# Eight batches of a transformer kernel: hardware loop on each engine, or the same body written out eight times

## The chip, the cores and the metric

The kernel runs on one core of a Trainium2 chip. The metric is device microseconds (us) of one execution, lower is better. Runs shown are several executions of the same program; one more execution was profiled and gives the trace.

## The reference, cut to what matters

Eight independent batches of 256 queries (128 features) pass through two layers. The first layer is a cross-attention over a context of 1601 rows and a mixture of nine experts, of which two are taken per query; the second is a cross-attention over 64 gathered context rows per query and a mixture of eight experts, of which two are taken, plus a shared one.

```
x = x + xattn0(layernorm(x), ctx)             # softmax over 1601 keys, 16 heads of 8
x = x + ffn0(layernorm(x))                    # 9 experts, hidden 352, top 2 by sigmoid
x = x + xattn1(layernorm(x), ctx, indices)    # softmax over 64 gathered keys
x = x + ffn1(layernorm(x))                    # 8 experts, hidden 176, top 2, and a shared one
```

The two attentions and the two mixtures are the same for every batch, with the same weights. Nothing flows from one batch to the next.

## The kernel before, in words

The program is written by hand for five instruction streams: `@block.sync` (SP, it only issues DMAs and keeps the books), `@block.tensor` (PE), `@block.scalar` (ACT), `@block.vector` (DVE) and `@block.gpsimd` (POOL). Each stream has a preamble that loads and transposes the weights and prepares batch 0, and then a loop of eight passes (`Fori(0, NB)`, L334, L767, L944, L1208, L1343), one batch a pass. Every pass has the same instructions at the same tiles; only SP's body uses the loop's index, for addresses in HBM (the inputs of the batches after this one, L338 and L342, and the output of this one, L353).

Within a pass PE does, in order: the row maxima of the first attention against all 1601 keys (`max_part`, L455, two matmuls a part, each part read by a DVE reduction, L1054), transposes of the next batch's context among them (`context_T`, L541), scores and weighting (L477, L493), counts of the gathered indices (`count`, L550, many tiny matmuls), the first mixture (`experts`, L673), the second attention, the second mixture. The inputs of the next batch are prepared within the pass, so the next pass can begin at once with `max_part`. `keep_clock` (L397) issues matmuls whose result nobody reads, where PE would otherwise be idle; the last four of a pass stand at L803.

The passes are tied together by a meeting. The semaphores only count upward within a pass and are compared with constants, so they are cleared once a pass. PE, ACT, DVE and POOL each call `meet` at the end of a pass (L804, L953, L1225, L1356): drain the engine, add one to `met`, wait for the own `go` semaphore. SP waits in `close` (L318) for the last loads and for `met` to reach four, clears the semaphores and raises the four `go`. Before `close`, SP issues the store of the batch (L353), which it may do once DVE has added the last residual (L1171). After `go`, each engine clears its own `go` and then meets the loop's closing instructions: add one to a register, compare, branch back to the head of the body. The same `meet` and `close` stand once ahead of the loop (L332, L766, L943, L1207, L1342), and there the engines run on into the body without a backward branch.

```
def meet(eng, k):
    eng.drain().then_inc(met, 1)
    eng.wait_ge(go[k], 1)
    eng.sem_clear(go[k])
```

Of the kernel before, what the change touches and what calls it, by code (L numbers as in the profile page):

```python
# [28 lines left out]
NB, NQ, D = 8, 256, 128  # L29
# [39 lines left out]
def build(nc, x, ctx_in, itok, Wq, bq, Wkv, bkv, Wo, bo, w1, w2, w3, nw1, nw2, nw3, gw, ngw, gb,  # L69
# [6 lines left out]
    with ExitStack() as es:  # L76
# [135 lines left out]
# [5 lines that stand above are left out]
# [39 lines left out]
        def _(sp):  # L256
            def load_x(b):
                sp.dma_start(xs[0][:, :, :], x[b].rearrange("a (s p) d -> p (a s) d", p=P)).then_inc(x_in, 16)
                sp.dma_start(idx_i[:, :, :], itok[b].rearrange("a (s p) k -> p (a s) k", p=P)).then_inc(idx_in, 16)

            def load_ctx(b):
                sp.dma_start(ctx_sb[:, 0:KC - 1, :],
                             ctx_in[b, 0:(KC - 1) * P, :].rearrange("a (c p) d -> p (a c) d", p=P)).then_inc(ctx_in_s, 16)
                sp.dma_start(ctx_sb[0:KLAST, KC - 1, :],
                             ctx_in[b, (KC - 1) * P:NK, :].rearrange("a k d -> (a k) d")).then_inc(ctx_in_s, 16)

            def spread(parts, scratch, dst, done, filled, ready):

                for t in range(3):
                    sp.wait_ge(ready, t + 1)  # L270
                    sp.dma_start(scratch[t], parts[t]).then_inc(done, 16)

                    sp.wait_ge(done, 16 * (t + 1))
                    src = scratch[t].rearrange("(a h d) k -> h d a k", h=2, d=HD)
                    for hh in range(2):
                        for term in range(NT):
                            if KPART[term] == t:
                                r = SLOT * hh + HD * term
                                sp.dma_start(dst[r:r + HD, :, 0:src.shape[3]], src[hh]).then_inc(filled, 16)
# [38 lines left out]
            def close():  # L318

                sp.wait_ge(kst_in, 16 * 2 * NT)  # L320
                sp.wait_ge(k1st_in, 16 * 2 * NT)
                sp.wait_ge(x_in, 16)
                sp.wait_ge(idx_in, 16)
                sp.wait_ge(ctx_in_s, 32)
                sp.wait_ge(met, 4)
                sp.sem_clear(round_sems)  # L326
                for g in go:
                    sp.sem_inc(g, 1)
# [2 lines left out]
            sp.wait_ge(ctx_in_s, 64)  # L331
            close()  # L332
            sp.sem_inc(out_stored, 16)
            with sp.Fori(0, NB) as i:  # L334
                nxt = bass.ds((i + 1) % NB, 1)

                sp.wait_ge(ctxT_ready, 4)
                load_ctx(bass.ds((i + 2) % NB, 1))  # L338

                sp.wait_ge(x_ready, 1)  # L340
                sp.wait_ge(cnt_psum, 1)
                load_x(nxt)  # L342

                sp.wait_ge(out_stored, 16)
                sp.sem_clear(out_stored)
                sp.sem_inc(xo_free, 1)

                sp.wait_ge(att_done, 1)
                spread(kpart, k_parts, kst, kw_done, kst_in, kp_ready)
                sp.wait_ge(att_done, 2)  # L350
                spread(kpart1, k1_parts, k1st, kw1_done, k1st_in, kp1_ready)
                sp.wait_ge(x_ready, 4)
                sp.dma_start(out[bass.ds(i, 1)].rearrange("a (s p) d -> p (a s) d", p=P), xs[4][:, :, :]).then_inc(out_stored, 16)  # L353
                close()
# [41 lines left out]
        def _(pe):  # L396
# [111 lines left out]
            def attention0():  # L508
                done = [0]

                def parts(upto):
                    while done[0] < min(upto, NH0):
                        max_part(done[0])
                        if 1 <= done[0] < START:
                            keep_clock(2, ob[:, :])
                        done[0] += 1
                for g in range(4):
                    parts(START + 2 * (g - CTX))
                    context_T(g)
                parts(START)  # L520
                pe.wait_ge(ctxT_ready, 4)
                for kind, n in fills0:
                    if kind == "q":
                        pair_queries(n, fill0[kind, n], m_ready, b_ready, b_read)
                    elif kind == "c":
                        if n == NP - 1:
                            for g in range(NP * NG - LAG, NP * NG):
                                weigh(g)
                            pe.wait_ge(part_read, NH0)
                            keep_clock(2)  # L530
                        combine(n, fill0[kind, n], oT_ready, b_ready, b_read)
                    elif n % 2 == 0:
                        g = n // 2
                        scores(g)
                        x = KC * (g // NG) + chunks(g % NG)[-1] + 1
                        parts(min(START + x * (PARTS + LEAD - START) // KC, LEAD + x * PARTS // KC))
                        if g >= LAG:
                            weigh(g - LAG)
                pe.drain().then_inc(att_done, 1)
# [224 lines left out]
            project(1, attT, wq_sb[:, :], True)  # L764
            all_queries(1, 0)
            meet(pe, 0)  # L766
            with pe.Fori(0, NB):  # L767
                attention0()
                keep_clock(2)
                count(0, COUNT[0])  # L770
                attend_T(0)
                keep_clock(2)
                count(COUNT[0], COUNT[1])
                attend_out(0, wo_sb[:, :])
                keep_clock(4)
                count(COUNT[1], COUNT[2])
                keep_clock(4)
                norm_T(1, False)
                keep_clock(2)
                count(COUNT[2], COUNT[3])  # L780
                experts(0)
                next_values(0, 2)
                mask_T()
                next_values(2, 4)
                norm_T(2, False)
                keep_clock(2)
                project(2, xnT, wq1T[:, :], False)
                keep_clock(8)
                all_queries(1, 1)
                keep_clock(3)  # L790
                attention1()
                keep_clock(3)
                attend_T(1)
                keep_clock(2)
                attend_out(1, wo1T[:, :])
                next_latent1()
                next_keys1()
                keep_clock(10)
                norm_T(3, False)
                keep_clock(2)  # L800
                experts(1)
                pe.wait_ge(hu_done[1], NC1)
                keep_clock(4)  # L803
                meet(pe, 0)  # L804
# [3 lines left out]
        def _(act):  # L808
# [132 lines left out]
            next_keys1()  # L941
            all_queries(0, 0)
            meet(act, 1)  # L943
            with act.Fori(0, NB):  # L944
                next_context()
                attention0()
                experts(0)
                next_values()
                attention1()
                next_keys1()  # L950
                experts(1)
                all_queries(2, 0)
                meet(act, 1)  # L953
# [3 lines left out]
        def _(dve):  # L957
# [247 lines left out]
            scale_queries(1, 0, st)  # L1205
            high_parts(st).then_inc(qres_ready, 1)
            meet(dve, 2)  # L1207
            with dve.Fori(0, NB):  # L1208
                st = Steps(dve, dve_step)
                attention0()  # L1210
                st.do(normalise(0, 0, H - 2, st))
                attend_out(0, x0b, xs[1], st)
                norm(1, xs[1], st)
                experts(0, xs[1], xs[2], st)
                norm(2, xs[2], st)
                scale_queries(1, 1, st)
                st.link(high_parts(st))
                low_parts(st)
                attention1(st)
                st.do(normalise(1, 0, H - 4, st))  # L1220
                st.do(normalise(1, H - 4, H - 2, st))
                attend_out(1, xs[2], xs[3], st)
                norm(3, xs[3], st)
                experts(1, xs[3], xs[4], st)
                meet(dve, 2)  # L1225
# [3 lines left out]
        def _(pool):  # L1229
# [110 lines left out]
            next_indices()  # L1340
            low_parts()
            meet(pool, 3)  # L1342
            with pool.Fori(0, NB):  # L1343
                st = Steps(pool, pool_step)
                attention0(st)
                rstd_of(1)
                next_keys()
                rstd_of(2)
                attention1(st)
                rstd_of(3)  # L1350
                next_keys1()
                next_x()
                rstd_of(4)
                next_indices()
                low_parts()
                meet(pool, 3)  # L1356
# [25 lines left out]
```

## Time and profile before

| | us |
|---|---|
| median of 3 runs | 1911.24 |
| lowest and highest run | 1907.75, 1912.42 |
| the profiled execution, its own time | 1908.32 |
| span of its trace, first to last instruction | 1906.5 |
| mean granted TensorE clock | 0.96 of full |
| body entered | 109.88 |

The profiled execution is 1.8 us longer than its span: that is what lies around the traced instructions. The trace has 36401 instructions. PE is the matmul part of TensorE and PEld its weight loads; SPq is the sequencer of SP. In the chain that ended last, "issue" is time for which the trace shows nothing that the engine waited for. The queues named "instruction" carry the code of the engines from HBM. The eight batches fill the span from 109.88 us to its end.

### The profile page before, as it was taken

The numbers are of one execution on the slowest core, as the hardware profiler recorded it, in microseconds if no ns is written. First come the engines' busy times: TensorE is split into PE (matmuls) and PEld (weight loads), VectorE is DVE, ScalarE is ACT, GpSimd is POOL, SyncE is SP. The second block draws the span as 40 slices with busy tenths as digits, with TensorE's granted clock in tenths as the row PEclk, the third lists the DMA queues.
The fourth block names the chain that finished last, engine by engine and source line by source line (L and its number), as shares of the span: only waits on it lengthen the run. The fifth ranks groups of instructions, "written<-read, shape, count | busy, mean of one in ns | idle before, by whom it ended". The sixth has DMA issues, their size and how long they took to land.

```text
span 1906.5 us, 36401 instructions
## 1 busy us (share of the span) xinstructions
PE 1667.5 (87%) x13858; PEld 905.6 (48%) x13858; DVE 1210.9 (64%) x2626; ACT 899.7 (47%) x2024; POOL 629.7 (33%) x1059
## 2 busy tenths in 40 slices
PE   4159998889988999899997899889998899989999
PEld 3113655237452474435652274534744346533655
DVE  4058555867468664795667764685747856578555
ACT  4138433572427534384335834276342753448433
POOL 3325223441324314352233513243142522335223
PEclk8679999899999999899999999999998999989999
DMA  7410130002200041000400022000311004000130
GB/s 207 76 32 2 30 53 17 19 2 49 35 17 19 6 65 26 24 2 18 66 13 22 2 41 44 17 19 6 59 22 33 2 6 75 17 23 2 30 54 16
DMA packets 56192, 60.30 MB, mean 32 GB/s; under 512 B 6437, under 2 KB 44209, under 8 KB 55985
## 3 DMA queue, kind: packets, MB, share of 16 engines
q1 hardware_dynamic: 55984, 57.57, 15.4%
q8 instruction: 127, 2.08, 0.4%
q14 instruction: 81, 0.66, 0.1%
HBM read 43.67 MB, written 13.88 MB: 30 GB/s over the span
## 4 chain that ended last, share of the span: by engine, by line
PE 69%; DVE 10%; issue 7%; ACT 6%; POOL 4%; DMA 3%; SPq 1%; another core or an unknown queue 0%; POOLq 0%
PE ob L700 7%; PE ob L503 7%; PE b L488 6%; PE a L687 6%; PE a L688 6%; PE a L464 4%; PE a L401 4%; PE b L473 4%; DVE mx L1054 3%; PE ob L401 3%; PE a L583 3%; PE a L582 3%; ACT probs L848 2%; PE b L694 2%; DMA k_parts<-big 2%
## 5 line engine op out<-in xcount | busy, mean ns | idle before, releaser
L1054 DVE TENSOR_REDUCE mx<-a 128x2 f32<-128x802 f32 (+1 forms) x512 | 497.8, 991 | 164.6 <-PE a L464 153.4
L848 ACT ACTIVATE probs<-b 128x512 f32<-128x512 f32 (+1 forms) x896 | 452.9, 567 | 50.1 <-PE b L488 43.3
L503 PE MATMUL ob<-probs,vaug 128*9 128x256 f32 (+1 forms) x3328 | 279.6, 389 | 17.7 <-ACT oT L810 17.7
L917 ACT ACTIVATE big<-a 128x256 f32<-128x256 f32 (+2 forms) x304 | 116.7, 384 | 304.7 <-PE a L688 304.0
L1276 POOL TENSOR_TENSOR big<-iotab,idx_lo 128x512 bf16<-128x512 bf16 x256 | 258.0, 1039 | 5.0
L464 PE MATMUL a<-kst,qa 64*128 64x401 bf16 (+1 forms) x1024 | 180.4, 359 | 74.6 <-SPq L326 42.4
L488 PE MATMUL b<-sq_nat,kst 64*128 64x256 bf16 (+1 forms) x1664 | 174.3, 282 | 20.0 <-ACT probs L848 9.6
L1146 DVE SCALAR_TENSOR_TENSOR big<-big,a 128x256 f32<-128x256 f32 (+2 forms) x304 | 127.1, 418 | 85.2 <-ACT big L917 84.0
L1265 POOL CAST qst<-nm 128x4 bf16<-128x4 f32 x64 | 12.8, 200 | 434.5 <-DVE nm L1038 434.5
L1232 POOL TENSOR_TENSOR rstd<-veps,neg_half 128x2 f32<-128x2 f32 x33 | 23.2, 704 | 361.1 <-DVE veps L965 361.1
L488 PEld LDWEIGHTS b<-sq_nat,kst 64*128 64x128 bf16 (+1 forms) x1664 | 51.4, 96 | 184.8 <-ACT probs L848 171.7
L401 PE MATMUL a<-identb 128*128 128x512 bf16 x496 | 133.5, 380 | 1.7
L1140 DVE TENSOR_TENSOR probs<-big,b 128x256 f32<-128x256 f32 (+2 forms) x304 | 125.8, 414 | 0.6
L1154 DVE TENSOR_TENSOR big<-big,a 128x256 f32<-128x256 f32 (+2 forms) x304 | 125.7, 413 | 0.0
L1066 DVE TENSOR_REDUCE mx<-a 128x4 f32<-128x1024 f32 x64 | 78.4, 1225 | 72.9 <-PE a L583 72.9
L700 PE MATMUL ob<-w2T,probs 128*128 128x128 f32 (+1 forms) x800 | 122.8, 276 | 1.6
L687 PE MATMUL a<-xnT,w1T 128*128 128x256 f32 (+1 forms) x400 | 121.2, 385 | 0.0
L503 PEld LDWEIGHTS ob<-probs,vaug 128*9 128x9 f32 (+1 forms) x3328 | 55.4, 88 | 137.8 <-ACT probs L848 55.8
L688 PE MATMUL a<-xnT,w3T 128*128 128x256 f32 (+1 forms) x400 | 119.0, 379 | 0.0
L700 PEld LDWEIGHTS ob<-w2T,probs 128*128 128x128 f32 (+1 forms) x800 | 105.3, 191 | 25.4 <-DVE probs L1140 4.7
L464 PEld LDWEIGHTS a<-kst,qa 64*128 64x128 bf16 x1024 | 52.2, 100 | 134.0 <-issue 97.0
L1288 POOL TENSOR_TENSOR probs<-probs,cntT 128x512 f32<-128x512 f32 x64 | 81.1, 1267 | 103.6 <-ACT probs L866 102.8
(220 smaller groups left out, 2655.7 us busy)
## 6 DMA issues: line engine op xcount, KB each, us to landing
kst<-k_parts SPq DMA_DIRECT2D x108, 200.1 KB
k_parts<-big SPq DMA_DIRECT2D x27, 400.2 KB, 14.2
ctx_sb<-in_ctx SPq DMA_DIRECT2D x10, 768.0 KB
k1st<-k_parts SPq DMA_DIRECT2D x108, 32.0 KB
k_parts<-kpart SPq DMA_DIRECT2D x27, 64.0 KB, 1.8
kst<-in_L_ffn_w SPq DMA_DIRECT2D x1, 1408.0 KB
x<-in_x SPq DMA_DIRECT2D x9, 128.0 KB, 2.1
out<-x SPq DMA_DIRECT2D x8, 128.0 KB, 1.8
```

Source lines behind the costliest of these rows:

```text
L401: pe.matmul(bank, identb[:, :], identb[:, :].unsqueeze(1).to_broadcast([P, 4, P]), start=True, stop=True)
L464: m = pe.matmul((a0, a1)[k % 2][:, hh * MMAX:hh * MMAX + n], qa[o:o + SLOT, p, s, :], kst[o:o + SLOT, p, j * KM:j * KM + n], start=True, s ...
L488: m = pe.matmul(bs[e[hh] % 3][0:kn, (c % 2) * NQ:(c % 2 + 1) * NQ], kst[o:o + SLOT, p, c * P:c * P + kn], qp[o:o + SLOT, p % 2, :], start= ...
L503: m = pe.matmul(ob[q:q + V1, 0:NQ], vaug[0:kn, c, 2 * p + hh, :], probs[0:kn, (2 * g + hh) % NPS, (c % 2) * NQ:(c % 2 + 1) * NQ], start=(j ...
L687: pe.matmul(gu_bank[c % 3][0:n, 0:NQ], wga[:, c * P:c * P + n], xnT[:, :], start=True, stop=True)
L688: pe.matmul(gu_bank[c % 3][0:n, NQ:2 * NQ], wua[:, c * P:c * P + n], xnT[:, :], start=True, stop=True).then_inc(gu_ready[l], 1)
L700: m = pe.matmul(ob[:, s * P:(s + 1) * P], hid[0:n, c % 4, s * P:(s + 1) * P], wda[0:n, c, :], start=(c == 0 and s == 0), stop=(c == nch - ...
L848: act.activation(probs[0:kn, n % NPS, 0:w], bs[e % 3][0:kn, 0:w], ACT.Exp).then_inc(b_read, 1)
L1054: dve.tensor_reduce(mx[:, p % 2, s, :, j], (a0, a1)[k % 2][:, :].rearrange("p (h k) -> p h k", h=2)[:, :, 0:n], AX, ALU.max, negate=True). ...
L1140: dve.tensor_tensor(hid[0:n, c % 4, :], hu[0:n, c % 3, :], cb_bank[c % 2][0:n, 0:NQ], ALU.mult).then_inc(hid_ready[l], 1)
L1146: dve.scalar_tensor_tensor(out=gt[0:n, c % 3, :], in0=th[0:n, c % 3, :], scalar=1.0, in1=g[0:n, 0:NQ], op0=ALU.add, op1=ALU.mult).then_inc ...
L1276: m = pool.tensor_tensor(onehot[:, q:q + QG, :], iotab[:, :].unsqueeze(1).to_broadcast([P, QG, P]), idx_lo[:, q:q + QG].unsqueeze(2).to_br ...
```

## The change

The five hardware loops become Python loops at build time. The body of each engine's loop stands eight times in a row in its instruction stream. The order of instructions, the tiles, the semaphores, the meeting and its clearing stay. On SP the index is now a number known at build time, so the addresses of the input and output DMAs are constants.

```diff
@@ sync
-            with sp.Fori(0, NB) as i:
+            for i in range(NB):
                 nxt = bass.ds((i + 1) % NB, 1)
@@ tensor
-            with pe.Fori(0, NB):
+            for _ in range(NB):
                 attention0()
@@ scalar
-            with act.Fori(0, NB):
+            for _ in range(NB):
                 next_context()
@@ vector
-            with dve.Fori(0, NB):
+            for _ in range(NB):
                 st = Steps(dve, dve_step)
@@ gpsimd
-            with pool.Fori(0, NB):
+            for _ in range(NB):
                 st = Steps(pool, pool_step)
```

## Rows read from the trace of the kernel before

**Rows 1.** The page, part 1: busy time of each engine over the span.

```profile
PE 1667.5 (87%) x13858; PEld 905.6 (48%) x13858; DVE 1210.9 (64%) x2626; ACT 899.7 (47%) x2024; POOL 629.7 (33%) x1059
```

**Rows 2.** Windows, one per batch (2, 5, 8) and all eight: length, busy times, clock.

```profile
335.41:561.09 225.68, 205.30 (x1713) 110.42 (x1714) 148.62 (x323) 109.11 (x248) 74.61 (x127) 0.97 0.13 26
...
1009.34:1233.12 223.78, 203.70 (x1712) 110.11 (x1713) 148.43 (x323) 109.02 (x248) 74.61 (x127) 0.98 0.14 26
...
1683.76:1906.50 222.74, 205.23 (x1712) 110.44 (x1712) 148.63 (x323) 109.10 (x248) 74.61 (x127) 0.98 0.13 26
sum 1796.62, PE 1638.74 PEld 882.80 DVE 1188.17 ACT 872.62 POOL 596.86; mean PE 204.84 PEld 110.35 DVE 148.52 ACT 109.08 POOL 74.61
```

**Rows 3.** Chain that ended last, whole span: start, length, its longest pieces without cause.

```profile
331.53 3.88 issue
...
556.85 4.24 issue
...
781.25 3.60 issue
...
1005.28 4.05 issue
...
1229.35 3.77 issue
...
1454.55 3.92 issue
...
1679.85 3.91 issue
```

**Rows 4.** The same chain close up, where batch 2 ends.

```profile
555.35 0.43 DVE x L1171
...
555.80 0.04 SPq L353
...
555.88 0.03 SPq L353
...
555.94 0.41 SPq L353
...
556.61 0.24 SPq L326
```

**Rows 5.** The same chain close up, where batch 1 is entered.

```profile
109.60 0.10 SPq L326
109.70 0.18 issue
109.88 0.85 PE a L464 x4
```

**Rows 6.** Waits of PE and PEld: total us, times, longest.

```profile
PE a L464 <- issue: 31.4, 7, 4.8
...
PEld ob L503 <- issue: 48.5, 189, 0.7
```

**Rows 7.** DMA queues, at one boundary (331.5 to 335.5), then within batch 2.

```profile
q8 instruction: 1, 0.02, 1.5%
...
q8 instruction: 15, 0.25, 0.4%
```

**Rows 8.** Windows after the first boundary; PEclk is the granted clock.

```profile
335.40:340.00 4.60, 4.59 (x16) 0.83 (x16) 3.67 (x4) 0.00 (x0) 0.00 (x0) 0.54 0.03 9
340.00:345.00 5.00, 5.00 (x30) 2.04 (x28) 4.68 (x7) 1.19 (x2) 0.41 (x2) 1.00 0.00 0
```

**Rows 9.** Timeline, first maxima of batch 2; in brackets idle time before, and its releaser.

```profile
335.41 0.85 PE L464 MATMUL a<-kst,qa 64*128 64x401 bf16 x4 [4.46 <-issue]
...
335.96 2.79 DVE L1054 TENSOR_REDUCE mx<-a 128x2 f32<-128x802 f32 x3 [5.52 <-PE a L464]
...
339.13 3.00 DVE L1054 TENSOR_REDUCE mx<-a 128x2 f32<-128x796 f32 x3 [0.37 <-PE a L464]
```

**Rows 10.** Timeline of PE: its densest run of instructions in batch 1.

```profile
204.73 1.65 PE L556 MATMUL b<-idx_c,big 128*128 128x4 bf16 x60
```

## The prediction

> **What bounds the kernel now.** I read the page's busy times first. TensorE is the busiest engine with 87% of the span, DVE has 64%, the others less [rows 1]. Five loops' closing instructions can't compete with that on average; the question is only what they do at the seam between two batches. So I next cut the span into batches: they take from 223.78 to 225.68 us, and the last, after which no branch goes back, takes 222.74 although its store's landing is in it [rows 2]. Third, the chain of work that ended last. Its longest pieces without a cause are seven, one at each seam, of 3.60 to 4.24 us; their sum is 27.37 us, or 3.91 each [rows 3]. There are seven backward branches in eight passes, and seven such pieces.
>
> Close up at the seam after batch 2, the chain runs through DVE's last residual (L1171), SP's steps for the store (L353) and the raising of `go` (L326), and then nothing for 4.24 us until PE's first maxima [rows 3, 4]. All four engines have been standing in `meet` until L326, so nothing they computed is late. The same meeting stands ahead of the loop, and there is the comparison that carries this prediction: from L326 to PE's first matmul it takes 0.18 us [rows 5]. Same drain, same wait, same clearing of `go`, same first matmul; the only thing missing is the branch back. PE's own waits say the same: seven waits for no visible cause ahead of L464, the longest 4.8 us, while in the middle of the body the most frequent wait of that kind is never over 0.7 us [rows 6].
>
> Why 3.9 us for a branch? The code queue shows it. The queue that I take for PE's (its 15 blocks of 0.25 MB / 15 = 17 KB within the 221 us of a batch are the most, and PE has the most instructions) gets one block within the 4 us of a seam [rows 7]. I read this as the head of the body being fetched from HBM again, with PE waiting. [...]
>
> **The change part by part.** (a) *The branch at seven seams, removed.* From `go` to first matmul 3.91 us become the 0.18 of the entry: 7 x 3.73 = 26.1 us, all on the chain. This gap is covered by nothing: PE, DVE, ACT and POOL do nothing else in it. The other four engines lose their branches too; those lie beside PE's, since DVE's first work of a pass follows PE's first matmul and ACT's and POOL's come later still, so they are costed at nothing. What would be late next at the seam is what remains: the last residual, then the store's issue, then `go`, about 1.5 us from L1171's start to L326's end [rows 4]. These stay.
>
> (b) *SP's index arithmetic, removed.* Ahead of the store's issue SP has two short steps of L353, at 555.80 and 555.88, before the DMA at 555.94 [rows 4]. They are the address in registers, or one of them is a wait. The bounds are 0 and 0.14 us a batch; I take 0.14, as both carry the store's line: 8 x 0.14 = 1.1 us. The loads' arithmetic (L338, L342) goes too, but SP then stands waiting for other engines most of the time, so that is nothing.
>
> (c) *The clock after the seam.* [...] PE had been idle for 4.46 us before it [rows 9]; without the branch that is 4.46 - 3.88 + 0.18 = 0.8 us, with matmuls dense behind it for 4.59 of 4.60 us [rows 8]. So I expect the clock not to fall there. What is that worth? Not half of the 4.6 us, since DVE's reductions pace this stretch: three in 2.79 us, then an idle 0.37 us waiting for PE, then three more in 3.00 [rows 9]. A full clock takes away that 0.37, and half of the 0.55 us between PE's first matmul and DVE's first reduction (335.41 to 335.96). That is 0.64 us a seam, 7 x 0.64 = 4.5. Bounds: nothing, if the clock falls all the same, and 4.5.
>
> (d) *The later dips of the clock.* The batches differ by up to 1.9 us with the same instructions [rows 2]. PE's busy time differs with them (203.70 against 205.30), and their mean clock (0.98 against 0.97), which is a short further stretch at the lower level. How these fall after the change I can't tell. Eight batches sum to 1796.62; without the last, seven average 224.84. All seven as the best (223.78) would give 7.4 us back, all as the worst (225.68) would cost 5.9 [rows 2]. I take nothing for them and keep both ends.
>
> (e) *Added: code is read straight on.* The stream is eight times as long in HBM, but a pass already reads its body afresh: 15 blocks in batch 2 [rows 7]. So the number of blocks hardly changes. What changes is where block borders fall: the same place in every pass before, eight different places after. A border costs something only if the engine runs through a block faster than the next arrives. In the densest stretch PE issues 60 matmuls of L556, each with its weight load, in 1.65 us [rows 10]. That is 120 instructions; a block holds some (1713 + 1714) / 15 = 228 of PE's [rows 2, 7], and the average block lasts 221 / 15 = 14.7 us [rows 7]. Against a fetch of at most some 4 us that is ample. Bounds 0 and 3.9 us a border; I take 0, by the longest wait of 0.7 us in the body, whose borders are read straight on too [rows 6].
>
> [...]
>
> *Sum.* 26.1 + 1.1 + 4.5 = 31.7 us. The profiled execution had 1908.3 with a span of 1906.5; it gives 1876.6. It lies 2.9 us under the median of the runs shown, 1911.24, so the median after should be about 1879.5.
>
> **The rivals.** *A: the gap is not the branch.* Something else at the seam, such as what clearing the semaphores or draining the engines leaves to do, takes the 3.9 us and stays. For it: seams and entry differ in that engines have just been at work. Against it: at the entry the same clearing and `go` give 0.18 us [rows 5], and the fetched block falls in the gap [rows 7]. Then only (b) is won: 1911.2 - 1.1 = 1910, within the noise. [...] 4%.
>
> *B: slower, by code that doesn't come in time.* The place is PE's stream at block borders in straight code, above all where the fetch shares the DMA engines with the spreading of keys. The price is up to 3.9 us a border. There are 15 borders a batch, 120 in all [rows 7]; with the 31.7 us won, it comes out slower from the ninth exposed border on (31.7 / 3.9 = 8.1). If two borders a batch were exposed, 16 x 3.9 = 62 us: 1879.5 + 62 = 1942. For it: the borders fall on new places, and blocks of other engines do so too. Against it: 15 borders in every pass now, none with a wait over 0.7 us, key spreading among them. 3%. With one to eight exposed borders it is a smaller gain, 1883 to 1911; I give that another 4%.
>
> *C: the gap goes, the clock gives nothing.* PE falls to the lower clock at the seam all the same, or later dips come in every batch. The branch's 26.1 and SP's 1.1 stay won: 1911.2 - 27.2 = 1884, and 1890 with the worst dips. For it: every seam and the entry start at the lower level. Against it: each of them follows 4 us or more without matmuls. 20%.
>
> **How the numbers follow.** My forecast, 1879.5 us, has 69%; C 20%, small gain 4%, A 4%, B 3%. The low end is the fastest run less the sum and the best of the dips: 1907.75 - 31.7 - 7.4 = 1868.7. The high end is the slowest run less (a) alone plus the worst dips: 1912.42 - 26.1 + 5.9 = 1892.2. That takes in C and leaves out A, B and most of the small gain, about 1 in 10, and the rest for what I mis-sized. A measurement of this kernel can tell about 0.3% (5.7 us) from no change: faster than 1905.5 needs only a fifth of the sum. So faster 0.94, same 0.04, slower 0.02.
>
> **What the changed profile would show.** The seven long "issue" pieces of the chain are gone, and L326 to L464 takes about 0.2 us at every seam; if pieces of 3 us or more stand there still, A is right. PE's waits for no visible cause ahead of L464 stay under 1 us. The short steps of L353 on SP vanish. The clock reads 1.0 in the first 5 us of batches 2 to 8; if about 0.5, C is right. The batches come out near 220 us each. The number of PE's code blocks stays near 15 a batch; new waits of 1 to 4 us for no visible cause within a body, at a different place in each batch, would be B.

## The result, and the profile after

The changed kernel takes 1862.8 us (median of 4 runs, 1860.5 to 1863.8); the one before took 1910.35 us in the same session (1907.75 to 1912.42). The ratio is 0.975, 95% interval 0.9733 to 0.9767. It is faster by 47.5 us, where 31.7 us were forecast, and the time lies 6 us below the forecast's range.

The page of the changed kernel: busy times, the granted clock in 40 slices, and the code queues.

```profile
span 1858.8 us, 36224 instructions
PE 1646.0 (89%) x13858; PEld 903.6 (49%) x13858; DVE 1207.0 (65%) x2626; ACT 899.6 (48%) x2024; POOL 631.2 (34%) x1059
...
PEclk9579999999999999999999999999999999999999
...
q8 instruction: 110, 1.80, 0.4%
q14 instruction: 61, 0.50, 0.1%
```

PE's busy time fell from 1667.5 to 1646.0 us for the same 13858 matmuls [rows 1]. That is not a branch that went away; it is the same work at a higher clock. In the page's row of the granted clock every slice from the fourth on reads 9, where before the change four of those slices read 8.

The chain that ended last, close up at the seam behind batch 1, as in [rows 4]:

```profile
327.10 0.44 DVE x L1171
...
327.55 0.41 SPq L353
...
328.21 0.23 SPq L326
328.45 0.09 issue
328.54 0.36 PE a L464 x2
...
328.92 1.00 DVE mx L1054
```

From L326 to PE's first matmul it is 0.09 us, at each of the seven seams; before it was 3.60 to 4.24 [rows 3]. Two short steps of L353 are gone from SP. PE's waits say it in one line, where there were seven waits for no visible cause ahead of L464 [rows 6]:

```profile
PE a L464 <- SPq L326: 45.7, 8, 42.1
```

The trace of the kernel before has rows for the branches themselves, at the lines of PE's loop (L767) and DVE's (L1208). PEldq and DVEq are the sequencers of the two engines, and the three numbers are the shortest, median and longest of eight, in ns. PE's took 3.6 us in the median and 79 ns at the shortest, which is the last one, where nothing goes back; DVE's took at most 72 ns:

```profile
L767 PEldq COMPARE_BRANCH  x8: 79/3645/3989, 331.7 to 1905.3; - x8
L1208 DVEq COMPARE_BRANCH  x8: 55/63/72, 331.8 to 1905.4; - x8
```

So nearly all of the gap at the seam lies inside PE's own branch instruction.

Windows by batch, as in [rows 2] (batches 2, 4 and 7, and the sum of eight; each begins at PE's first matmul of the batch):

```profile
328.54:546.62 218.08, 201.35 (x1713) 110.02 (x1714) 147.97 (x323) 109.03 (x248) 74.78 (x127) 1.00 0.13 26
...
764.68:983.87 219.19, 202.61 (x1712) 110.12 (x1713) 148.27 (x323) 109.09 (x248) 74.78 (x127) 0.99 0.14 26
...
1420.00:1639.43 219.43, 203.84 (x1712) 110.39 (x1713) 147.99 (x323) 109.05 (x248) 74.78 (x127) 0.98 0.13 26
...
sum 1750.36, PE 1617.73 PEld 880.66 DVE 1184.29 ACT 871.63 POOL 598.26; mean PE 202.22 PEld 110.08 DVE 148.04 ACT 108.95 POOL 74.78
```

Windows of the first 4.5 us of batch 2, as in [rows 8], and the timeline there, as in [rows 9]:

```profile
328.54:333.00 4.46, 4.03 (x21) 1.01 (x22) 4.08 (x5) 0.00 (x0) 0.00 (x0) 1.00 0.10 28
```

```profile
328.54 0.52 PE L464 MATMUL a<-kst,qa 64*128 64x401 bf16 x4 [0.51 <-SPq L326]
...
328.92 7.28 DVE L1054 TENSOR_REDUCE mx<-a 128x2 f32<-128x802 f32 x8 [1.40 <-PE a L464]
```

The clock stands at 1.00 where it read 0.54, and DVE makes its eight reductions in 7.28 us without a pause.

**Where the 47.5 us come from.** I cut each batch at four marks of the timeline: the start of DVE's second residual (L1171, the batch's end), PE's first maxima (L464), POOL's first use of a maximum (L1265), and the transposition of the attention's output (L445). Means over batches 2 to 8, in us. Both kernels were run and profiled a second time. The column "L464 to L445" is the first attention and holds the column before it; seam, first attention and the stretch behind it add up to the batch.

| | seam, L1171 to L464 | L464 to L1265 | L464 to L445 | L445 to next L1171 | batch |
|---|---|---|---|---|---|
| before | 5.41 | 9.18 | 91.63 | 127.77 | 224.80 |
| before, again | 5.33 | 9.09 | 92.11 | 127.77 | 225.21 |
| after | 1.44 | 7.94 | 89.23 | 127.75 | 218.42 |
| after, again | 1.44 | 7.93 | 89.18 | 127.77 | 218.39 |

The seam gives 3.9 to 4.0 us a batch, the first attention 2.4 to 2.9, everything behind it nothing at all. The gain of the first attention has two parts: 1.2 us up to L1265, where the clock is low behind the seam, and 1.2 to 1.8 us behind L1265. The second part is later dips of the clock. In batch 2 of the kernel before there were two, 14.5 and 21.3 us behind the first maxima:

```profile
349.90:353.30 3.40, 3.21 (x26) 0.98 (x30) 2.09 (x3) 2.43 (x6) 0.00 (x0) 0.50 0.58 169
...
356.70:360.10 3.40, 3.31 (x26) 0.98 (x30) 1.91 (x3) 1.82 (x5) 3.32 (x5) 0.50 0.00 0
```

The lower level of the clock reads 0.50 in both.

The second pair of profiles accounts for the medians' difference: 7 x (225.21 - 218.39) = 47.7 us. The first pair gives 7 x 6.38 = 44.7 and 2.9 us more in the preamble.

### The profile page after: what moved, and what is told of

It reads as the page before. It is cut to its first block, busy times and chain, and to the rows that moved or that the text cites. A ratio compares the mean times of both kernels' runs of the same rounds, so it can differ in the third digit from the quotient of the medians.

```text
span 1858.8 us, 36224 instructions
## 1 busy us (share of the span) xinstructions
PE 1646.0 (89%) x13858; PEld 903.6 (49%) x13858; DVE 1207.0 (65%) x2626; ACT 899.6 (48%) x2024; POOL 631.2 (34%) x1059
## 4 chain that ended last, share of the span: by engine, by line
PE 69%; DVE 11%; ACT 6%; issue 6%; POOL 4%; DMA 3%; SPq 1%; another core or an unknown queue 0%; POOLq 0%
PE ob L700 7%; PE ob L503 7%; PE b L488 6%; PE a L687 6%; PE a L688 6%; DVE mx L1054 4%; PE a L401 4%; PE a L464 4%; PE b L473 4%; PE a L583 3%; PE ob L401 3%; PE a L582 3%; ACT probs L848 3%; PE b L694 2%; DMA k_parts<-big 2%
## 5 line engine op out<-in xcount | busy, mean ns | idle before, releaser
L464 PE MATMUL a<-kst,qa 64*128 64x401 bf16 (+1 forms) x1024 | 172.2, 340 | 50.0 <-SPq L326 45.7
L1265 POOL CAST qst<-nm 128x4 bf16<-128x4 f32 x64 | 13.0, 203 | 388.8 <-DVE nm L1038 388.8
L1071 DVE TENSOR_TENSOR probs<-probs,cntT 128x512 f32<-128x512 f32 x64 | 44.3, 692 | 90.5 <-ACT probs L866 90.5
```

What stands on the lines that cost most here:

```text
L464: m = pe.matmul((a0, a1)[k % 2][:, hh * MMAX:hh * MMAX + n], qa[o:o + SLOT, p, s, :], kst[o:o + SLOT, p, j * KM:j * KM + n], start=True, s ...
```

## The experiments

**The two kernels again.**

> The kernel before once more, with a profile of its own. Its profiled batches 2 to 8 average 224.80 us, which with 218.42 after the change gives 44.7 us, 3 us short of the medians' difference of 47.5. If the looped kernel's later clock dips vary between executions, this profile shows another mean, up to 225.3; if the preamble carries the 3 us, the first maxima of batch 1 begin near 110 us here and near 107 with the code written out.

Measured 1909.49 us, and batches of 225.21. Its seven seams, from the chain that ended last:

```profile
331.61 3.74 issue
...
556.91 3.58 issue
...
782.14 3.56 issue
...
1007.41 3.95 issue
...
1232.79 3.87 issue
...
1458.06 4.22 issue
...
1682.48 3.87 issue
```

They average 3.83 us, so the first profile's 3.91 was typical.

The changed kernel again:

> The changed kernel once more, with a profile of its own. If the written-out code makes the preamble faster, the first maxima of batch 1 begin near 107 us again; if that was this execution's luck, they begin between 107 and 110. The batches 2 to 8 take 218.07 us, or up to 1.4 more where a short dip of the clock falls into one.

Measured 1863.67 us. Its first maxima begin at 110.45 us, as against 107.00 in the first profile of the same kernel and 109.88 and 109.99 in the two of the looped one. So the preamble's 2.9 us in the first pair were luck of one execution. In either profile five of batches 2 to 8 took 218.05 to 218.09 us; the other two had a short dip of the clock worth 1.1 to 1.4 us.

**PE alone written out.**

```diff
-            with pe.Fori(0, NB):
+            for _ in range(NB):
```

> Only PE's stream is written out; SP, ACT, DVE and POOL keep their loops. Theory (each engine that branches back waits some 4 us for its code, all five beside one another): PE starts 0.1 us after go, but DVE's first reduction then comes some 4 us after go, PE stops after two parts of maxima, and little is won: 1887 to 1903 us. Rival (as I predicted: the branches of the other four lie beside PE's and cost nothing): 1863 us, the same as with all five written out.

Measured 1895.9 us (ratio to before 0.992, 0.9903 to 0.9936). The chain at the first seam:

```profile
333.43 0.24 SPq L326
333.67 0.09 issue
333.76 0.53 PE a L464 x4
334.29 2.72 issue
337.01 1.01 DVE mx L1054
```

PE starts after 0.09 us, does two parts of maxima, and then the chain has 2.72 us of nothing until DVE's first reduction. DVE's own branch back takes the place of PE's (the wait stands behind the branch here, which itself lasts no longer than 72 ns). The batches average 222.85 us: a seam of 1.59, the first reduction 3.06 us behind PE's first matmul (0.39 with all written out), and a first attention of 93.11, which is 3.9 longer than with all written out, more than the 2.7 us of delay. PE stands still for 3 us behind its first parts, and a few us later the clock falls: in each of batches 2 to 8 a stretch at half the clock, of 3.4 us or more, begins 3.4 to 5.4 us behind the first maxima. So my cost of zero for the other four holds only because all of them lost the branch together. What ACT's, POOL's and SP's branches would cost alone was not tried.

**All but PE written out.**

```diff
-            for _ in range(NB):
+            with pe.Fori(0, NB):
```

> SP, ACT, DVE and POOL are written out; PE alone keeps its loop. Theory (PE's branch alone is enough to hold the seam): go to PE's first matmul stays 3.6 to 4.2 us and the lower clock stays behind it, so 1905 to 1910 us; SP's index steps are gone, which is 1 us. Rival (the gap comes from several engines fetching code at once): PE's gap shortens to 2 us or less and the time falls to 1890 or lower.

Measured 1908.3 us (0.9992, 0.998 to 1.0003): no difference from before. PE's waits:

```profile
PE a L464 <- issue: 28.8, 7, 4.2
```

The seam keeps 5.05 us and the first attention 92.44. PE's branch alone costs as much as all five together, as near as these runs can tell (0.9 us). These two kernels also tell whose queue is whose: with PE alone written out q8 carries 110 blocks and q14 80; with PE alone looping they are 127 and 62. So q8 is PE's, as I had taken it.

**Keep the gap, keep TensorE working in it.**

```diff
                 keep_clock(4)
                 meet(pe, 0)
+                keep_clock(16)
```

> All five loops stay as before; PE gets 16 matmuls of keep_clock after its meeting at the end of each pass, queued ahead of the branch, so that the array works while the branch waits for code (3.4 us of matmuls at the full clock). Theory (the idle gap lets the clock fall, and the lower clock costs 2.4 us a batch in the first attention): the gap stays but the clock behind it reads 1.0, and 7 x 2.4 = 17 us are won: 1893 us. Rival (the lower clock behind the seam costs nothing beyond the 0.64 us a seam that I predicted, or does not come from the gap): 1906 to 1911 us.

Measured 1895.28 us (0.9924, 0.9905 to 0.9944), 14 us won against the 17 expected, with every loop in place. The timeline of PE at the first seam, and the windows behind it:

```profile
331.66 3.62 PE L401 MATMUL a<-identb 128*128 128x512 bf16 x16 [0.67 <-SPq L326]
335.49 0.52 PE L464 MATMUL a<-kst,qa 64*128 64x401 bf16 x4 [0.20 <-issue]
```

```profile
335.49:340.00 4.51, 4.08 (x21) 1.05 (x22) 4.13 (x5) 0.00 (x0) 0.00 (x0) 1.00 0.03 7
```

The 16 matmuls run while the branch waits for its code, 16 in 3.62 us (ten of them took 2.32 us in the kernel before, at the full clock); the branch itself lasts as long as before:

```profile
L767 PEldq COMPARE_BRANCH  x8: 79/3468/3895, 331.9 to 1889.8; - x8
```

The seam stays at 5.35 us, varying from 5.15 to 5.72 (5.05 to 5.73 in the looped kernel), so it is not the matmuls that fill it up. But the clock behind it reads 1.00, and the first attention takes 89.07 us, as in the changed kernel. One batch of seven was 2.8 us longer in its second half, with a dip of the clock in the middle of busy work. The six others average 222.05 us, 3.2 under the looped kernel's 225.21, which is somewhat more than the theory's 2.4.

**Keep the code written out, put a gap back.**

```diff
                 sp.dma_start(out[...], xs[4][:, :, :]).then_inc(out_stored, 16)
+                sp.wait_ge(out_stored, 16)
+                sp.dma_start(out[...], xs[4][:, :, :]).then_inc(out_stored, 16)
+                sp.wait_ge(out_stored, 32)
                 close()
```

(The waits and increments for `out_stored` elsewhere go from 16 to 32.)

> All written out, as in the change, but SP waits at each seam for the store to land, stores once more, and waits again before it raises go: an idle stretch of about 4 us with no branch and no code to fetch. Theory (the clock falls because TensorE stands idle, whatever the cause): 7 x (4.2 + 2.4) + 2 = 48 us over the change, 1911 us, the clock near 0.5 behind each seam, as before the change. Rival (the lower clock belongs to the branch or the fetch): only the 4.2 us, 1894 us, the clock near 1.0.

Measured 1902.47 us (0.9957, 0.994 to 0.9973). The chain at the seam and the windows behind it:

```profile
327.71 1.84 DMA out<-x
...
329.58 1.85 DMA out<-x
...
331.44 0.25 SPq L326
331.69 0.09 issue
331.78 0.84 PE a L467 x4
```

```profile
331.78:336.40 4.62, 4.62 (x18) 0.92 (x18) 3.73 (x5) 0.00 (x0) 0.00 (x0) 0.63 0.01 2
```

The seam is 4.51 us, 3.07 more than in the changed kernel (not 4.2, since the waits replace steps of SP). The first attention goes back to 91.59 us, 2.4 more, and the clock to 0.63 for 4.6 us. 7 x (3.1 + 2.4) = 38 us and 2 for the last store give the 39.7 us by which it is slower. There is no branch back in this kernel. Together the two experiments settle it: the 2.4 us belong to TensorE's idleness, not to the branch.

**Two batches in a body.**

```diff
-            with pe.Fori(0, NB):
+            with pe.Fori(0, NB // 2):
+                for _ in range(2):
```

(the same on the others; on SP the index is twice the turn plus the half)

> Four passes of a loop whose body holds two batches, on all five engines. Theory (the price is paid once for each backward branch: 4.0 us of seam and 2.4 us of lower clock): three such seams in place of seven, 1862.8 + 3 x 6.4 = 1882 us, with batches 3, 5 and 7 some 224 to 225 us long and batches 2, 4, 6 and 8 some 218 to 219. Rival (it is the written-out stream as a whole that runs better, or the order in which the blocks fall): no such alternation of the batches.

Measured 1884.29 us (0.9866, 0.985 to 0.9882). By the timeline batches 3, 5 and 7 take 223.98, 225.44 and 225.33 us, with seams of 4.94 to 5.43; batches 2, 4, 6 and 8 take 218.22, 220.50, 218.20 and 218.19, with seams of 1.59 to 1.61. The price is paid once a branch. Batch 4 is the exception in its second part: its seam is short, but two later dips of the clock made its first attention 91.13 us, 2.3 more than in the other even batches (88.84). The seams without a branch are 0.15 longer than in the changed kernel: SP's two steps are back.

**Loops with the branch's target fetched ahead.**

```diff
-            with pe.Fori(0, NB):
+            with pe.bass.Fori(0, NB, engines=[pe.engine], hint_back_edge=True):
```

```profile
329.84 0.24 SPq L326
330.08 0.83 issue
330.91 0.36 PE a L464 x2
```

PE's branch instruction, which took 3.6 us in the median, now takes 0.35:

```profile
L767 PEldq COMPARE_BRANCH  x8: 88/352/490, 330.3 to 1868.3; - x8
```

The hint is an instruction of its own at the head of each pass, at the same line on PE:

```profile
L767 PEldq BRANCH_PREFETCH_HINT  x8: 31/31/45, 108.6 to 1649.2; - x8
```

The code queue shows the target fetched ahead. In the kernel before, a block of q8 begins inside PE's branch at each of the seven seams, 1.0 to 1.6 us into it (at 333.03, the branch from 331.72 to 335.35). With the hint none begins inside any of the seven, nor behind it before PE's first matmul: the last block ahead of the seam begins 4.4 to 4.6 us ahead of the branch (at 325.70, the branch at 330.27, PE's first matmul at 330.91; from 326.2 to 331.4 q8 carries nothing). In the kernel before one begins 4.1 to 4.7 us ahead too, and the branch still waits for another. What the first matmuls need was there when the branch was taken.

The loop is the same but for the hint, and the 3.9 us are now 0.83, so the gap was the fetch of the body's head. The clock stays up: first attention 89.31. What remains is 0.82 us of seam a batch more than the written-out code, 5.7 us in all; more dips of the clock (four of batches 2 to 8 have one in the first attention, one of them a further one behind it; the runs spread from 1873.9 to 1886.1); and the end of the kernel. From the last L1171 to the end of the span it is 4.98 us, with the code written out 2.70 and in the plain loops 2.85. DVE's last branch, which is not taken, is over at 1868.47 us, and its next instruction starts at 1871.29. That the code behind the loop has to be fetched there is the likely reason; it wasn't tried.

**The store behind close.**

```diff
+                close()
                 sp.dma_start(out[...], xs[4][:, :, :]).then_inc(out_stored, 16)
-                close()
```

> All written out, and SP issues the store of the batch behind close instead of ahead of it. Theory (SP's steps are what is left of the seam, 1.44 us of which the store's issue is 0.41): the seam falls to about 0.9 us and the time by 7 x 0.5, less 0.5 at the very end where the store now starts later: 1860 us. Rival (the engines' drain sets go, not SP): no change, 1863 us.

Measured 1863.07 us (0.9746, 0.9729 to 0.9762 against before): no change from 1862.8. The chain at its first seam:

```profile
328.77 1.10 DVE x L1171
329.87 0.21 SPq L326
330.08 0.09 issue
330.17 0.36 PE a L464 x2
```

What was SP's 0.41 us is now DVE's: from L1171's start it is 1.10 us until `met` is complete and L326 can run. The seam falls from 1.44 to 1.39 only. The rival was right: two paths of nearly the same length lead to `go`, and I had looked at the one that the chain shows.

**The hint and the store behind close together.**

> The hinted loops on all five engines, and the store behind close. The two parts should add: 1878.1 - 3.5 = 1874.6 us if the store's issue lies on the seam there too; 1878 if the branch (0.8 us from go to PE's first matmul with the hint) hides it.

Measured 1874.13 us (0.9814, 0.9798 to 0.983). The seam went from 2.26 to 2.07 us, which is 1.3 us of the 3.9 by which the medians differ; the rest is within the spread of the hinted kernel's runs. This one stays inconclusive.

**A warm entry.**

```diff
             all_queries(1, 0)
+            pe.wait_ge(kw1_done, 16)
+            keep_clock(20)
             meet(pe, 0)
```

> The changed kernel, and PE issues 20 matmuls of keep_clock ahead of its first meeting, once the first part of the second layer's keys has been written to HBM (some 10 us before go). Theory (the entry into batch 1 pays the same price for TensorE's idle 42 us as the seams did for their gap): the clock behind the entry reads 1.0, batch 1's first attention takes about 89 us in place of 92.3, and the time falls by 3 to 3.5 us to 1860 us. Rival (batch 1 is slow for another reason): its first attention stays at 92 us, and the time at 1863 us.

Measured 1860.74 us (0.9743, 0.973 to 0.9756; 1860.17 to 1861.79). Windows ahead of the entry (PE's first maxima begin at 109.59) and behind it:

```profile
105.00:109.60 4.60, 1.65 (x10) 0.56 (x8) 0.00 (x0) 0.00 (x0) 0.00 (x0) 1.00 0.14 43
109.60:111.70 2.10, 1.72 (x10) 0.43 (x10) 1.72 (x2) 0.00 (x0) 0.00 (x0) 0.99 0.04 12
111.70:115.10 3.40, 3.40 (x11) 0.57 (x10) 2.96 (x4) 0.00 (x0) 0.00 (x0) 0.50 0.00 0
```

Half a success: the clock is full at the entry, where in the changed kernel it read 0.50 for the first 3.4 us, but 2.1 us later it falls once, for 3.4 us. PE had stood idle for 2.95 us between its 20 matmuls and the entry; whether the fall comes of that wasn't tried. Batch 1's first attention takes 90.07 us in place of 92.34, and that is the 2 us by which the median is lower. It is the fastest version I ran, though 2 us is less than these runs can tell with certainty.

## Why the prediction was wrong, step by step

The terms of the prediction beside what the two pairs of profiles show (before less after, seven batches), in us:

| term | forecast | first pair | second pair |
|---|---|---|---|
| (a) and (b), the seam | 27.2 | 27.8 | 27.2 |
| (c), L464 to L1265 | 4.5 | 8.7 | 8.1 |
| (d), later dips, L1265 to L445 | 0 | 8.1 | 12.4 |
| preamble, batch 1 and end | 0 | 3.0 | -0.5 |

The failed step is the price of the clock: (c) was costed at about half of what it is worth, and (d) was put at nothing. Together they were 4.5 us in the sum, and 16.8 and 20.5 were measured. Even their two upper ends, 4.5 and 7.4, come to only 11.9.

**(a) The branch: right.** 3.73 us a seam were forecast, 3.82 measured in the first profile (3.91 to 0.09). The entry's 0.18, which I took as what would remain, holds a step of the loop too: one instruction of 33 ns on PE at L767, which the written-out code doesn't have. The comparison of seam and entry carried the term.

**(b) SP's index steps: right.** The start of L353's DMA moved from 0.59 to 0.45 us behind L1171's start, which is the 0.14.

**(e) Straight code: right.** The stretch from L445 to the next L1171 takes 127.77 us before and 127.75 after, though its block borders fall elsewhere in each batch: the first block of PE's code that starts 4 us or more behind the first maxima does so 11.9 to 12.9 us behind them in batches 2 to 8 before, and 4.7 to 20.1 us after. Rival B did not occur anywhere. The blocks of code fell from 127 to 110 and from 81 to 61; I had expected no change.

**(c) The clock behind the seam: right mechanism, wrong size.** I priced the 4.6 us at 0.54 of the clock at 0.64 us a seam, with nothing and 4.5 us in all as bounds. The stretch that I looked at, L464 to L1265, shortened by 1.2 us. I had counted the one idle piece of DVE that [rows 9] show. The next row of that timeline has a second one, of 0.17 us:

```profile
342.29 1.89 DVE L1054 TENSOR_REDUCE mx<-a 128x2 f32<-128x802 f32 x2 [0.17 <-PE a L464]
```

And three reductions in 3.00 us is not DVE's own pace. When PE is never late they follow one another every 0.91 us (eight in 7.28), though each lasts 0.99 by the page. The upper bound was wrong as well: a wait counted from one row is no upper bound for a clock.

**(d) The later dips: wrong in their cause, and put at nothing.** I took them for a matter of chance that could fall either way, with 7.4 us to be won at best. For the most part they follow the gap. With the gap gone, or filled with matmuls, five of seven batches have none; with the gap put back by other means they return (91.59 us). Over all profiles but that of PE alone written out, counted from batch 2 on, 30 of the 31 batches behind a gap of 4 us without matmuls have a dip that begins 12 to 23 us behind the first maxima, and 19 of the 53 others have one too. So a part of them is chance, as I had said, and what calls them forth where there was no gap stays open. Even the best batch before, whose 90.74 us from L464 to L445 my low end was built on, was 1.9 us slower than the undisturbed 88.87. No batch before showed the full clock's time, so the best of them was no floor. The windows of [rows 2] also hold the seam behind each batch, which varied from 5.10 to 5.73 us, so not all of their spread was the clock's.

A bound was to be had from [rows 2]. A mean clock of 0.97 over 225.68 us is up to 6.8 us of clock lost a batch. Part of that is lost in the gap, where nobody needs it, and part hides behind DVE: in [rows 8] 0.46 x 4.6 = 2.1 us of clock are lost behind the seam, and L464 to L1265 shortened by 1.2. But 6.8 was the honest upper end of (c) and (d) together for such a batch, and it would have put the low end of the range at 1907.75 - 27.2 - 7 x 6.8 = 1833.

**The rivals.** A (the gap isn't the branch) fell with the result, with the 3.6 us that PE's branch instruction lasts, and again with the hinted loops. B fell as said. C (the clock gives nothing), to which I had given 20%, was wrong to the other side.

## What to carry to other kernels

In this kernel the backward branch cost more than its wait: 3.9 us of fetching plus 2.4 to 2.9 us because TensorE comes back at the lower clock, 0.54 of full over the first 4.6 us. PE and DVE both pay, 3.6 to 4.2 us and 2.4 to 2.7, beside one another, so undoing one branch won less than its price: PE's alone won 13 of the 47 us, and undoing all but PE's won nothing that these runs can tell. Where the code can't be written out, the hint is the next best: it won two thirds here, 31 us, and filling the gap with queued matmuls won 14. On PE the wait showed in the branch instruction's own row of the trace (3.6 us in the median); on DVE it stood behind a branch of at most 72 ns, as time without a cause. When a stall of the busiest engine is removed, bound the clock's share by the mean clock of the whole batch, not by one idle piece behind the stall.

## What was unexpected of the hardware

- A gap of some 4 us does not only lower the clock behind it. In the looped kernel six of batches 2 to 8 in the first profile and all seven in the second had a further dip or two at half the clock, of 3.4 us each, during the next 25 us, in the changed one two of seven have a single one, of 3.4 or 6.8 us; that is 1.2 of the 2.4 us in the first pair of profiles and 1.8 of the 2.9 in the second.
- DVE's branch back, with PE's code written out, leaves 2.4 to 2.7 us of nothing on the chain, PE's 3.6 to 4.2. PE's wait is inside its branch instruction (3.6 us), DVE's stands behind a branch of at most 72 ns. The blocks differ in size: 1.80 MB in 110 blocks on PE's queue is 16 KB each, 0.50 MB in 61 on the other instruction queue, q14, 8 KB. Whether that is the cause wasn't tried, nor does a run show whose queue q14 is.
- With the hint on all engines, queue q14 carried 8 blocks in all, as against 81 in the loops without it and 61 written out. Why stays open.
- Five times in all profiles a batch took 2.7 to 2.8 us longer behind L445, once with PE alone written out in batch 1 and once in batch 8, and in one batch each with the matmuls in the gap, with the hint and with the gap put back. In all five the clock reads half for 6.8 us, some 151 to 155 us behind the first maxima, amid busy matmuls. Why is open; the two profiles each of the kernel before and of the changed kernel have none.
